# Read-backs of the stacked queries and keys: six transfers of whole rows in place of sixteen pieces

## The reference

```python
x = _L0_xattn_ref(x, ctx, mask, ...)        # 16 heads of 8, cross-attention, post-norm
x = _L1_xattn_ref(x, ctx, ...)              # causal self-attention, cross-attention, top-2 of 8 experts
x = _L2_xattn_ref(x, ctx, ...)              # 8-bit quantised self- and cross-attention, gated feed-forward
x = _L3_xattn_ref(x, ctx, mask, ...)        # 16 heads of 64 with 4 key/value heads, feed-forward

Q  = (q_in @ wq + bq).reshape(Bq, Sq, H, HD)          # H = 16, HD = 8
Kp = (k_in @ wk + bk).reshape(Bq, Sk, H, HD)
scores = jnp.einsum('bqhd,bkhd->bhqk', Q, Kp) / jnp.sqrt(jnp.float32(HD))
a = jax.nn.softmax(scores, axis=-1)
o = jnp.einsum('bhqk,bkhd->bqhd', a, V)
```

## Time and profile before

| | us |
|---|---|
| median of three runs | 1616.45 (1616.28 to 1617.36) |
| profiled execution, its time | 1629.24 |
| profiled execution, its span | 1627.4 |
| PE busy | 1109.7 (68%) |
| DVE busy | 1109.3 (68%) |
| ACT busy | 895.0 (55%) |
| POOL busy | 681.6 (42%) |

### The profile page before, as it was taken

The page is one execution under the profiler, slowest core; times in us unless marked ns, Lnnn a source line. Parts: engine busy times, 40 slices in busy tenths (PEclk is TensorE's granted clock), DMA queues, the critical chain, the costliest instruction groups (busy, mean ns, idle before and its releaser), DMA issues.

```text
span 1627.4 us, 28786 instructions
## 1 busy us (share of the span) xinstructions
PE 1109.7 (68%) x9344; PEld 600.2 (37%) x9344; DVE 1109.3 (68%) x3126; ACT 895.0 (55%) x2546; POOL 681.6 (42%) x1054
## 2 busy tenths in 40 slices
PE   2688888787777679784435354444439787898888
PEld 1333344444322238681111121122215544453545
DVE  2577777777666666277989899877765556666533
ACT  1344455545543346347767688888872344545542
POOL 3321010111011323456888888877771245354420
PEclk9899999999998999796555555555559889999999
DMA  6223242022172111217546566655650112111000
GB/s 175 62 47 72 49 120 92 10 72 48 32 150 42 35 41 52 74 40 182 116 95 111 97 110 118 120 109 107 106 106 1 26 40 53 33 28 46 3 1 26
DMA packets 263829, 115.86 MB, mean 71 GB/s; under 512 B 216056, under 2 KB 252544, under 8 KB 261504
## 3 DMA queue, kind: packets, MB, share of 16 engines
q1 hardware_dynamic: 258720, 107.61, 31.6%
q0 software_dynamic: 2048, 4.20, 0.9%
q10 hardware_dynamic: 2912, 2.22, 0.5%
HBM read 38.80 MB, written 16.45 MB: 34 GB/s over the span
## 4 chain that ended last, share of the span: by engine, by line
PE 35%; POOL 19%; issue 17%; DVE 15%; ACT 10%; DMA 2%; SPq 1%; POOLq 0%; another core or an unknown queue 0%; ACTq 0%; DVEq 0%
POOL arena L2268 10%; ACT arena L1562 5%; PE acc L1177 3%; PE trans L1149 2%; POOL inv_total L2257 2%; PE misc L999 2%; PE misc L1005 2%; PE trans L1301 2%; ACT arena L1509 2%; POOL arena L2215 2%; PE score L1313 2%; PE score L1315 2%; PE trans L1155 2%; PE acc L1175 1%; DVE arena L1727 1%
## 5 line engine op out<-in xcount | busy, mean ns | idle before, releaser
L2268 POOL TENSOR_SCALAR arena<-arena,inv_total 128x512 f16<-128x512 f32 (+1 forms) x512 | 302.6, 591 | 55.8 <-DVE inv_total L2038 15.4
L1960 DVE TENSOR_REDUCE minus_top<-score 128x4 f32<-128x616 f32 (+4 forms) x256 | 201.4, 803 | 140.9 <-PE score L1110 54.6
L2134 POOL TENSOR_TENSOR rstd<-spread,minus_half 128x4 f32<-128x4 f32 x36 | 37.7, 1048 | 526.1 <-DVE spread L1643 456.9
L1562 ACT ACTIVATE arena<-score,minus_top,exp_scale 128x512 f32<-128x512 f32 (+1 forms) x340 | 210.6, 626 | 18.1 <-POOL arena L2268 8.1
L1509 ACT ACTIVATE arena<-trans 128x512 f32<-128x512 f32 x240 | 134.5, 596 | 113.8 <-PE trans L1155 107.8
L1600 ACT ACTIVATE arena<-arena,minus_top 128x154 f32<-128x154 f32 x256 | 105.1, 412 | 133.0 <-DVE minus_top L2103 132.9
L1258 PE MATMUL score<-arena 32*128 32x512 bf16 (+1 forms) x340 | 69.0, 458 | 144.1 <-ACT arena L1562 143.2
L2044 DVE TENSOR_REDUCE top_score<-score 128x2 f32<-128x1024 f32 (+1 forms) x128 | 135.7, 1061 | 0.6 <-PE score L1258 0.5
L2288 POOL TENSOR_TENSOR arena<-arena,inv_total 128x512 f32<-128x512 f32 x64 | 66.7, 1041 | 147.4 <-DVE inv_total L2111 133.6
L1562 ACT ACTIVATE arena<-trans,minus_top,exp_scale 128x154 f32<-128x154 f32 (+1 forms) x172 | 105.6, 621 | 16.2 <-POOL arena L2268 11.8
L2098 DVE CUSTOM_DVE_ANT_0 arena<-score,arena 128x154 f32<-128x154 f32 x256 | 66.0, 314 | 62.8 <-PE score L1338 62.4
(11 more groups left out here) (282 smaller groups left out, 2902.6 us busy)
## 6 DMA issues: line engine op xcount, KB each, us to landing
arena<-q_terms SPq DMA_DIRECT2D x176, 64.0 KB
late<-arena SPq DMA_DIRECT2D x128, 64.0 KB, 2.0
q_terms<-arena SPq DMA_DIRECT2D x36, 128.0 KB
late<-k_terms SPq DMA_DIRECT2D x64, 64.0 KB
arena<-arena SPq DMA_TRANSPOSE x192, 3.1
by_expert<-zeros SPq DMA_DIRECT2D x2, 1472.0 KB, 17.6
arena<-by_expert SPq DMA_DIRECT2D x10, 256.0 KB, 3.0
from_expert<-arena SPq DMA_DIRECT2D x10, 256.0 KB
```

Source lines behind the costliest of these rows:

```text
L1562: ins = nc.scalar.activation(probs[:, i % 3, j, of], quant_score[i % 3][:, j, of], ACT.Exp, bias=minus_top[:, at_col:at_col + 1], scale=ex ...
L1960: nc.vector.tensor_reduce(dst, src, axis=AX.X, op=ALU.max, negate=True).then_inc(top_ready, 1)
L2268: ins = nc.gpsimd.tensor_scalar(codes[:, (i - 1) % CODE_SOURCES, j, to], probs[:, (i - 1) % 3, j, of], inv_total[:, at_col:at_col + 1], HA ...
```

## The change

The three constants `Q_TERMS`, `K_TERMS` and `STACK` become `TERMS = 3`, `STACK = 64` and three reads of each side a half. The scratch tensors in DRAM get the term as their outermost index, so that a half's 8 features of one term are 64 KB in one piece. The order of the 8 products becomes (q0 k0), (q0 k1), (q0 k2), (q1 k0), (q1 k1), (q1 k2), (q2 k0), (q2 k1): for the keys the terms run 0, 1, 2, 0, 1, 2, 0, 1, for the queries each term is repeated. So three products are read in one transfer: 24, 24 and 16 rows for each half, six transfers for each side of a unit, with the same 128 rows of the same bytes. The writes remain three for each side. The waits count 6 transfers instead of 16. The matmuls stay as they were.

```diff
-Q_TERMS = [0, 0, 1, 0, 2, 1, 1, 2]
-K_TERMS = [0, 1, 0, 2, 0, 1, 2, 1]
-STACK = len(Q_TERMS) * HD
+TERMS = 3
+STACK = (TERMS * TERMS - 1) * HD
+K_READS, Q_READS = 3, 3
...
-        scratch = {side: nc.dram_tensor(f"{side}_terms", [2 * HD, 3, PAIRS, TOKENS], bf16)
+        scratch = {side: nc.dram_tensor(f"{side}_terms", [TERMS, 2 * HD, PAIRS, TOKENS], bf16)
...
+        def key_reads(keys, terms):
+            flat = keys.rearrange("p c k -> p (c k)")
+            for half in range(2):
+                of = terms[:, half * HD:(half + 1) * HD, :, :].rearrange("t d c k -> t d (c k)")
+                for n in range(TERMS):
+                    at, times = half * STACK + n * TERMS * HD, TERMS - n // 2
+                    yield flat[at:at + times * HD], of[0:times]
+        def query_reads(queries, terms):
...
+                    yield flat[at:at + times * HD], of[n].unsqueeze(0).to_broadcast([times, HD, of.shape[2]])
...
-                        for s in range(2):
-                            for n, term in enumerate(K_TERMS):
-                                r = slice(s * STACK + n * HD, s * STACK + (n + 1) * HD)
-                                sp.dma_start(keys[r, :, :], k_terms_of[s * HD:(s + 1) * HD, term, :, :])\
-                                    .then_inc(k_stacked, 16)
+                        for dst, src in key_reads(keys, k_terms_of):
+                            sp.dma_start(dst, src).then_inc(k_stacked, 16)
...
-                            sp.dma_start(terms_of[:, t, :, :].rearrange("r c k -> c r k"), parts[side][:, t, 0:wide])\
+                            sp.dma_start(terms_of[t].rearrange("r c k -> c r k"), parts[side][:, t, 0:wide])\
```

More of the change, by code:

```diff
@@ L582, in build @@
         up_bank = [score[0][:, 0, :], score[0][:, 1, :], score[1][:, 0, :], score[1][:, 1, :]]
-        scratch = {side: nc.dram_tensor(f"{side}_terms", [2 * HD, 3, PAIRS, TOKENS], bf16)
+        scratch = {side: nc.dram_tensor(f"{side}_terms", [TERMS, 2 * HD, PAIRS, TOKENS], bf16)
                    for side in "qk"}
-        k_terms_ctx = nc.dram_tensor("k_terms_ctx", [2 * HD, 3, PAIRS, P + 32], bf16)
+        k_terms_ctx = nc.dram_tensor("k_terms_ctx", [TERMS, 2 * HD, PAIRS, P + 32], bf16)
         by_expert = [nc.dram_tensor(f"by_expert{g}", [EXPERT_BLOCKS * P, D], fp32) for g in range(2)]
@@ L706, in build @@
         FIRST_SEQUENCE_LOADS, REST_LOADS = 4, 2
+        def key_reads(keys, terms):
[6 more added lines that the diff above has]
+        def query_reads(queries, terms):
+            flat = queries.rearrange("p c k -> p (c k)")
+            for half in range(2):
+                of = terms[:, half * HD:(half + 1) * HD, :, :].rearrange("t d c k -> t d (c k)")
+                for n in range(TERMS):
+                    at, times = half * STACK + n * TERMS * HD, TERMS - n // 2
+                    yield flat[at:at + times * HD], of[n].unsqueeze(0).to_broadcast([times, HD, of.shape[2]])
         with nc.Block() as once:
@@ L796, in read_keys @@
                             sp.wait_ge(scoresT_ready, FIRST_SLOT[u - 1])
-                        for s in range(2):
-                            for n, term in enumerate(K_TERMS):
-                                r = slice(s * STACK + n * HD, s * STACK + (n + 1) * HD)
-                                sp.dma_start(keys[r, :, :], k_terms_of[s * HD:(s + 1) * HD, term, :, :])\
-                                    .then_inc(k_stacked, 16)
-                    def read_queries(pairs, stacked):
[L804 to L808, removed]
+                        for dst, src in key_reads(keys, k_terms_of):
+                            sp.dma_start(dst, src).then_inc(k_stacked, 16)
+                    def read_queries(pairs, stacked):
+                        for dst, src in query_reads(q_stack[:, u % 2, pairs, :], scratch["q"].ap()[:, :, pairs, :]):
+                            sp.dma_start(dst, src).then_inc(stacked, 16)
                     for side in "kq":
                         wide, terms_of = (width, k_terms_of) if side == "k" else (TOKENS, scratch["q"].ap())
-                        terms, done, stacked = (K_TERMS, k_out, k_stacked) if side == "k" else (Q_TERMS, q_out, q_stacked)
+                        reads, done, stacked = (K_READS, k_out, k_stacked) if side == "k" else (Q_READS, q_out, q_stacked)
                         sp.wait_ge(parts_ready, 2 * u + (1 if side == "k" else 2))
                         if u:
-                            sp.wait_ge(stacked, 16 * 2 * len(terms) * u)
-                        for t in range(3):
-                            sp.dma_start(terms_of[:, t, :, :].rearrange("r c k -> c r k"), parts[side][:, t, 0:wide])\
+                            sp.wait_ge(stacked, 16 * 2 * reads * u)
+                        for t in range(TERMS):
+                            sp.dma_start(terms_of[t].rearrange("r c k -> c r k"), parts[side][:, t, 0:wide])\
                                 .then_inc(done, 16)
@@ L1086, in scores_exact @@
                     if i == 0:
-                        pe.wait_ge(k_stacked, 32 * len(K_TERMS) * (u + 1))
+                        pe.wait_ge(k_stacked, 32 * K_READS * (u + 1))
                         if u:
-                            pe.wait_ge(q_stacked, 32 * len(Q_TERMS) * (u + 1))
+                            pe.wait_ge(q_stacked, 32 * Q_READS * (u + 1))
                         else:
-                            pe.wait_ge(q_first, 32 * len(Q_TERMS))
+                            pe.wait_ge(q_first, 32 * Q_READS)
                         if stage(u) == L0:
@@ L1096, in scores_exact @@
                     if u == 0 and i == PER_GROUP[0]:
-                        pe.wait_ge(q_stacked, 32 * len(Q_TERMS))
+                        pe.wait_ge(q_stacked, 32 * Q_READS)
                     if at_step >= 2:
@@ L1489, in _ @@
                 act.wait_ge(k_out, 48)
[L1490 to L1494, removed]
+                for dst, src in key_reads(k_stack_ctx[:, 0, :, :], k_terms_ctx.ap()):
+                    act.dma_start(dst, src).then_inc(k_stacked, 16)
                 item("tops", 0, 0)
@@ L2173, in item @@
                     elif name == "kt":
-                        pool.wait_ge(k_stacked, 32 * len(K_TERMS) * (u + 1))
+                        pool.wait_ge(k_stacked, 32 * K_READS * (u + 1))
                         two = k_stack_ctx[:, u % 2, :, :].rearrange("p (g z) k -> p g z k", z=2)
```

## The result

The changed kernel takes 1661.67 us (median of 4 runs, 1652.80 to 1672.71) where the kernel before took 1616.37: 1.0273 times as long, 95% interval 1.0229 to 1.0318. Forecast were 1634.8 in a range to 1662.0; the direction and the mechanism were right, the size was not: +45.3 us where +18.3 was forecast. The profiled execution, the slowest of the four, took 1672.71 us with a span of 1670.9, 43.5 more than before. On another chip the same pair took 1657.87 and 1625.87 us, 32.0 apart: there the excess over the forecast is about half as large.

A forecast was written before the change was run, and what follows sets the result against it. TensorE was taken as busiest, with its waits for query read-back on the path at 8 of 12 units. Unit delays summed to +18.3 us on 1616.45, giving 1634.8 us, range 1610 to 1662.

The forecast's parts named there:

- How many engines a read runs on: Merged reads: the smaller outermost count decides, so the 24, 24 and 16 row reads run on 3, 3 and 2 engines.
- Price of a row, 0.32: Read-back: one engine moves an 8 KB row in 0.32 us, the full-load rate; bounds 0.32 and 0.88.
- Issue to first score: First key read's issue to first score: 23.2 us in cross-attention units, 33.8 us in units 5 to 7.
- The sum: Delays at the units' first scores added up, counted in full: +18.3 us.
- The writes keep 8 engines and their 0.6 us of issue: Term writes to DRAM, all units: unchanged by the merged reads, so no time added.
- its keys being read 19 us earlier: Unit 4: only query reads count before its first score, 193.0 instead of 191.28, +1.7 us.
- Unit 0, 0.1 us: Unit 0's query reads: landing at 43.3 instead of 43.16, +0.1 us; saved SyncE issues give nothing.
- Unit 9, -0.6: Unit 9's first score at 459.9 instead of 460.50, -0.6 us; weight loads behind its reads merely finish later.
- Unit 8, covered: Unit 8's first score is 33.2 us behind its keys' issue and needs 23.2, so no delay.
- Rival 1: Merged reads spread over eight or more engines, making the kernel faster: 1587 us taken, chance 0.12.
- Rival 2: Reads on three engines, but rows dearer than 0.32 us; at 0.36, +27 us to 1662; chance 0.14.
- Rival 3: Delays at units' starts are taken up by TensorE's later waits; time 1617 us, chance 0.08.

The follow-up runs named there:

- the run on eight engines: Changed kernel's six reads a side, but with the feature outermost in DRAM's access and stack rows in that order; 0.9711 times the kernel before, 1581.45 us.
- The changed kernel's second profile: The changed kernel run again, unedited, on another chip; 1.0185 times the kernel before there.

## Why the forecast was right in kind and short in size

- *How many engines a read runs on*: right, 3, 3 and 2, shown by the 16 marks and by the run on eight engines.
- *Price of a row, 0.32*: right; 3 engines at 70 GB/s give 0.35 with the pauses at either end. Issue to first score: 23.2 forecast, 24.1, 23.7 and 24.0 in units 1 to 3, 23.9 and 23.9 in units 10 and 11; 33.8 forecast, 33.6, 34.6 and 33.7 in units 5 to 7.
- *The sum* failed in the terms of units 0, 4 and 9, which are 19.2 us together where 1.2 was forecast. "The writes keep 8 engines and their 0.6 us of issue" left out that three of these eight are now busy with key rows (in the trace from 21.85 to 30.46 us in unit 0, from 179.15 to 197.16 in unit 4), so that the query terms land 3.2 us later in each. For unit 4 the step "its keys being read 19 us earlier" counted its key reads as off the path; yet their rows end after the query terms' writes are issued at 192.03. Added there 6.6 us, not 1.7: these 3.2, and 3.4 more from the first query read to the score (19.3 us, where the forecast had 17.6 and the kernel before 15.9).
- *Unit 0, 0.1 us*: 8.4. Its first query read comes 4.7 us later: 3.2 for these writes to land, 1.1 as they begin later, 0.4 as their issue takes longer. From that read to the second part's landing it is 20.9 us (30.38 to 51.28), not 17.6, and 17.4 before. I had said that the issues lie beside moving data; for 2 KB rows they don't: six reads issued at 0.71 us apiece are 4.3 us, their 48 rows at 0.08 only 3.8. And the weights of the queue behind are among the 6 KB rows: 128 packets of 4 KB and 520 of 512 B, 55.3 us of packet time, which is 3.5 us an engine by estimate, if all 16 share them evenly. These parts are read from the trace and were not tried one by one. (SyncE saves 20 issues here, not 26.)
- *Unit 9, -0.6*: 4.2; I had said that the loads behind its reads are merely late themselves. They hold up its rows by 4.5 us, as the run with the loads one unit later shows.
- *Unit 8, covered*: it never waits, yet added 3.0. From unit 7's first score to unit 8's it is 55.3 us in eight of the ten profiles, 56.8 in one, and 58.4 in this one, where the granted clock of the stretch is 0.94 instead of 1.00 and TensorE is busy 3.05 us longer with the same work: a matter of that execution. The changed kernel's second profile has 55.35. The stretch in the kernel before, then in the changed one:

```profile
361.34:416.67 55.33, 44.61 (x634) 24.13 (x629) 41.19 (x90) 29.07 (x55) 5.39 (x8) 1.00 0.19 36
```
```profile
392.03:450.40 58.37, 47.66 (x631) 25.22 (x632) 41.29 (x90) 28.47 (x54) 5.39 (x8) 0.94 0.10 34
```
- *Rival 1* (wide spread) was false for this kernel. The run on eight engines shows what it is worth: 47.5 us below the kernel before, where I had priced it at 29, at most 40, and at 18 for eight engines with the row at 0.88 us. The row was 0.44. The 0.88 was read as the rate of eight engines that write neighbouring partitions in step, though unit 6 in the earlier trace rows has eight engines writing neighbouring partitions at 0.36.
- *Rival 2* (1662) met the measured 1661.67 by luck: its reason, dearer rows, is false. *Rival 3* fell: no unit caught up, and the lag grows from 8.4 us at unit 1's key reads to 41.5 at unit 11's first score.

## What to carry to other kernels

Before merging transfers, read off how many engines each will run on: count completion marks (packets of a few bytes) in a window with one kind of transfer, and compare the DMA share. A merged transfer whose outermost index on either side is small is moved by few engines, and here the writes that needed those engines waited there too. Put the larger index outermost, on both sides, before counting issues saved.

## What the runs showed of the hardware

- Eight engines writing pieces of eight neighbouring partitions took 0.88 us for an 8 KB row in unit 2 of the kernel before, but 0.39 in unit 1 and 0.36 in unit 6, and 0.39 behind key reads on three engines (155 GB/s over 7.4 busy engines). To partitions 8 apart, issued more slowly, the row took 0.41; in transfers of up to three rows an engine 0.44. What makes the difference is not shown.
- A read's issue on SyncE's queue took 0.34 us for 8 partitions next to each other, 0.58 for 8 partitions 8 apart, and 0.71 on average over the reads of 24, 24 and 16.
- TensorE's granted clock fell to 1.2 GHz within idle stretches. In the changed kernel's wait before unit 1's first score (78.08 to 90.95 us, TensorE idle) it goes from 2.4 GHz (0.99) to 1.2 (0.50):

```profile
78.10:82.10 4.00, 0.00 (x0) 0.00 (x0) 0.00 (x0) 1.28 (x3) 3.32 (x9) 0.99 0.19 80
82.20:90.90 8.70, 0.00 (x0) 0.00 (x0) 0.00 (x0) 0.00 (x0) 1.62 (x4) 0.50 0.13 46
```

The mean is 0.92 in the changed kernel's first 650 us and 0.98 in the first 600 us of the run on eight engines, where the earlier trace rows has 0.94:

```profile
0.00:650.00 650.00, 455.94 (x4414) 214.04 (x4415) 401.95 (x997) 274.48 (x502) 99.20 (x156) 0.92 0.20 65
```
```profile
0.00:600.00 600.00, 466.16 (x4632) 236.40 (x4659) 422.39 (x1071) 296.65 (x561) 107.51 (x163) 0.98 0.25 73
```

What of the 41.5 us is due to the clock was not tried by itself; unit 8's 3.0 is where it shows alone.
